# FP4 feed-forward: rounding shared by VectorE and ScalarE, gate and up products in halves around the turning of the tile two behind

## Chip, cores and metric

One core of one Trainium2 chip. The metric is the device time of one execution in microseconds (us); lower is better.

## What is computed

Two transformer layers on 4 x 1024 tokens of width 256, each a residual sum: local attention and a mixture of eight experts, then a delta-rule attention and a feed-forward with weights and activations rounded to FP4. The change touches the last of the four only:

```python
def fp4_quant_dequant(x):                     # blocks of 16 along the last dim
    xb = x.reshape(shape[:-1] + (shape[-1] // 16, 16))
    scale = jnp.maximum(jnp.max(jnp.abs(xb), axis=-1, keepdims=True) / 6.0, 1e-12)
    xn = xb / scale
    idx = jnp.searchsorted(_MID, jnp.abs(xn)) # 0, .5, 1, 1.5, 2, 3, 4, 6
    return (_GRID[idx] * jnp.sign(xn) * scale).reshape(shape)

def fp4_linear(x, w):
    return jnp.einsum('bsk,nk->bsn', fp4_quant_dequant(x), fp4_quant_dequant(w))
...
x = x + _L1_ffn_ref(_layernorm(x, axis=-1), L1_ffn_w_gate, L1_ffn_w_up, L1_ffn_w_down)
# _L1_ffn_ref: fp4_linear(silu(fp4_linear(x, w_gate)) * fp4_linear(x, w_up), w_down); 704 hidden columns
```

## The kernel before

`fp4_feed_forward` first runs the three earlier stages and then its own block, with one instruction list for each engine; semaphores tie the lists together, and each list runs in the order written. The weights have been rounded and packed before. The 4096 tokens are 32 tiles of 128 tokens (`NT`), in 8 trips of 4 (`TRIPS`, `UN`); the tiles of a trip are called tile 0 to 3 here, and n counts tiles through all trips.

Once a trip, for all four tiles together (1024 columns, "wide"): VectorE takes the statistics of the next trip's input (`norm`, L1961, after the hidden product of tile 0), GpSimd the reciprocal root (L1929), VectorE normalises and finds block scales, ratio, exponent and `zmagic` (`round_z`, L1972 to L1988, after tile 1), and GpSimd adds `zmagic`, subtracts it and multiplies by the scale (L1931 to L1935). Adding and subtracting a number of the right size rounds the ratio to FP4's steps. TensorE turns the rounded tiles against the identity (`transpose_z`, L2064, in tile 3) and ScalarE copies them out of PSUM (`copy_zT`).

For each tile n: TensorE makes the gate and up products in two halves of 352 columns (`gate_up`, L2074); ScalarE takes the silu of each half (`silus`); VectorE multiplies silu and up (`hidden`, L1990) and rounds the 704 columns to FP4 (`round_h`, with `fp4`, L1942 to L1959: nine instructions, each waiting for the one ahead). TensorE turns the rounded tile in six pieces (`transpose_h`, L2086), ScalarE copies it out (`copy_hT`), TensorE multiplies by the down weights (`down`, L2095) and VectorE adds the residual into y (`result`, L2002), which the sync queue stores. TensorE's list is: gate and up of n, turning of n - 1, down product of n - 1. VectorE's is: result of n - 2, hidden of n, rounding of n. All is 32-bit float; in the traces each such product stands as two matmul instructions.

Of the kernel before, what the change touches and what calls it, by code (L numbers as in the profile page):

```python
# [14 lines left out]
P = 128  # L15
D = 256
# [1840 lines left out]
def fp4_feed_forward(nc, x_in, consts, w, x_out, T, I):  # L1857
# [21 lines left out]
    with ExitStack() as stack:  # L1879
# [42 lines left out]
        @block.gpsimd  # L1922
        def _(pool):
            pc = Chain(pool, pool_chain)
            blocks = lambda a: a.rearrange("p (b e) -> p b e", e=FP4_BLOCK)
            pool.wait_ge(loaded, 32)
            for t in range(TRIPS):
                pool.wait_ge(var_ready, t + 1)
                nc.gpsimd.tensor_tensor(rstd[:], ve[:], mhalf[:].to_broadcast([P, UN]), ALU.pow).then_inc(rstd_ready, 1)  # L1929
                pool.wait_ge(z_scaled, t + 1)  # L1930
                pc.link(nc.gpsimd.tensor_tensor(zlevel[:], zratio[:], zmagic[:], ALU.add))  # L1931
                pc.link(nc.gpsimd.tensor_tensor(zlevel[:], zlevel[:], zmagic[:], ALU.subtract))
                if t > 0:
                    pool.wait_ge(zT_psum, t * 2)
                nc.gpsimd.tensor_tensor(blocks(qz[:].rearrange("p u d -> p (u d)")), blocks(zlevel[:]),  # L1935
                                        zscl[:].unsqueeze(2).to_broadcast([P, WIDE // FP4_BLOCK, FP4_BLOCK]), ALU.mult).then_inc(qz_ready, 1)

        @block.vector
        def _(dve):
            c = Chain(dve, chain)  # L1940

            def fp4(n, cols, src, out, done, after_read=None):  # L1942

                nb = cols // FP4_BLOCK
                blocks = lambda a: a.rearrange("p (b e) -> p b e", e=FP4_BLOCK)
                per_block = lambda a: a[0:n, 0:nb].unsqueeze(2).to_broadcast([n, nb, FP4_BLOCK])
                r, e, mg, l = ratio[0:n, 0:cols], expo[0:n, 0:cols], magic[0:n, 0:cols], level[0:n, 0:cols]
                c.link(nc.vector.tensor_reduce(amax[0:n, 0:nb], blocks(src), AX, ALU.max, apply_absolute_value=True))  # L1948
                c.link(nc.vector.tensor_scalar(scl[0:n, 0:nb], amax[0:n, 0:nb], 1.0 / FP4_MAX, 1e-12, ALU.mult, ALU.max))
                c.link(nc.vector.reciprocal(inv[0:n, 0:nb], scl[0:n, 0:nb]))  # L1950

                ins = nc.vector.scalar_tensor_tensor(blocks(r), blocks(src), TIES_DOWN, per_block(inv), ALU.mult, ALU.mult)  # L1952
                c.link(ins)
                c.link(nc.vector.tensor_scalar(e.bitcast(U32), r.bitcast(U32), EXPONENT, None, ALU.bitwise_and))  # L1954

                c.link(nc.vector.tensor_scalar(mg, e, 1.0, HALF_STEP, ALU.max, ALU.mult))  # L1956
                c.link(nc.vector.tensor_tensor(l, r, mg, ALU.add))  # L1957
                c.link(nc.vector.tensor_tensor(l, l, mg, ALU.subtract))  # L1958
                nc.vector.tensor_tensor(blocks(out), blocks(l), per_block(scl), ALU.mult).then_inc(done, 1)  # L1959
# [12 lines left out]
            def round_z(t):  # L1972
                dve.wait_ge(rstd_ready, t + 1)
                for u in range(UN):
                    ins = nc.vector.tensor_scalar(z[:, u, :], x[:, t % XB, u, :], mv[:, u, 0:1], rstd[:, u:u + 1], ALU.subtract, ALU.mult)  # L1975
                c.link(ins)
                if t > 0:
                    dve.wait_ge(qz_ready, t)
                nb = WIDE // FP4_BLOCK
                blocks = lambda a: a.rearrange("p (b e) -> p b e", e=FP4_BLOCK)  # L1980
                src = blocks(z[:].rearrange("p u d -> p (u d)"))
# [3 lines left out]
                c.link(nc.vector.scalar_tensor_tensor(blocks(zratio[:]), src, TIES_DOWN, inv[:].unsqueeze(2).to_broadcast([P, nb, FP4_BLOCK]), ALU.mult, ALU.mult))  # L1985
                c.link(nc.vector.tensor_scalar(expo[:].bitcast(U32), zratio[:].bitcast(U32), EXPONENT, None, ALU.bitwise_and))
                nc.vector.tensor_scalar(zmagic[:], expo[:], 1.0, HALF_STEP, ALU.max, ALU.mult).then_inc(z_scaled, 1)
                dve.wait_ge(z_scaled, t + 1)  # L1988

            def hidden(n):  # L1990
                for j in range(2):
                    dve.wait_ge(silu_ready, n * 2 + j + 1)
                    ins = nc.vector.tensor_tensor(h[:, n % 2, j * HI:(j + 1) * HI], silu[:, n % 2, j * HI:(j + 1) * HI], ps_u[j][:, 0:HI], ALU.mult)  # L1993
                    ins.then_inc(h_ready, 1)
                dve.wait_ge(h_ready, n * 2 + 2)

            def round_h(n):
                if n >= 2:
                    dve.wait_ge(hT_psum, n - 1)
                fp4(P, I, h[:, n % 2, :], qh[:, n % 2, :], qh_ready)  # L2000

            def result(n):  # L2002
                t, u = divmod(n, UN)
                dve.wait_ge(y_psum, n + 1)
                if t > 0:
                    dve.wait_ge(stored[u], 16 * t)
                nc.vector.tensor_tensor(y[:, u, :], ps_y[:, 0:D], x[:, t % XB, u, :], ALU.add).then_inc(y_ready, 1)

            norm(0)
            round_z(0)  # L2010
# [10 lines left out]
            result(NT - 2)  # L2021
            result(NT - 1)

        @block.scalar
        def _(act):
# [6 lines left out]
            def silus(n):  # L2032
                if n >= 2:
                    act.wait_ge(h_ready, 2 * n - 2)
                for j in range(2):
                    act.wait_ge(gu_psum, n * 2 + j + 1)
                    nc.scalar.activation(silu[:, n % 2, j * HI:(j + 1) * HI], ps_g[j][:, 0:HI], ACT.Silu).then_inc(silu_ready, 1)
# [9 lines left out]
            for p in range(2):  # L2047
                copy_zT(0, p)
            for n in range(NT):
                t, u = divmod(n, UN)  # L2050
                silus(n)
                if n >= 1:
                    copy_hT(n - 1)
                if u == 3 and t + 1 < TRIPS:
                    for p in range(2):
                        copy_zT(t + 1, p)
            copy_hT(NT - 1)

        @block.tensor
        def _(pe):  # L2060
# [3 lines left out]
            def transpose_z(t):  # L2064
                for p in range(2):
                    pe.wait_ge(qz_ready, t + 1)
                    pe.wait_ge(zT_ready, t * 2 + p)
                    for u in (2 * p, 2 * p + 1):
                        for k in range(KD):
                            col = ((u - 2 * p) * KD + k) * P  # L2070
                            ins = nc.tensor.transpose(ps_z[:, col:col + P], qz[:, u, k * P:(k + 1) * P], ident[:])
                    ins.then_inc(zT_psum, 1)

            def gate_up(n):  # L2074
                t, u = divmod(n, UN)
                pe.wait_ge(zT_ready, t * 2 + u // 2 + 1)
                for j in range(2):
                    if n >= 1:
# [85 lines left out]
```

## Time and profile before

| | us |
|---|---|
| median of 3 runs | 3606.68 (3600.88 to 3606.81) |
| profiled execution | 3596.48 |
| its span, first to last instruction | 3594.6 |
| mean granted clock of TensorE | 0.952 |
| feed-forward stage in the span | 3200 to 3594.6 |

Busy over the whole span: TensorE 3199.4 us (89%), VectorE 2525.7 (70%), ScalarE 1396.1 (39%), GpSimd 945.4 (26%). These shares mix four stages; the feed-forward has to be read by itself. In the rows PE is TensorE, PEld its weight loads, DVE VectorE, ACT ScalarE, POOL GpSimd; L is a line of the kernel. A granted clock of 1.00 is 2.4 GHz for the whole stretch, 0.50 would be 1.2 GHz. Matmuls overlap in the records, so their pace is read from start to start.

### The profile page before, as it was taken

Reading aid. Unit: us, or ns where it says so; the run is one execution under the profiler, and the core shown is the slowest. Engines: PE = TensorE matmul, PEld = TensorE weight load, DVE = VectorE, ACT = ScalarE, POOL = GpSimd, SP = SyncE. Lnnn points to the kernel's source line nnn. Section 1 sums busy time; section 2 is a strip of 40 time slices with the busy share of each in tenths; the row PEclk is TensorE's granted clock in tenths of the full one; section 3 lists DMA queues with packets and bytes.
Section 4 is the critical chain, followed back from the end, with each engine's and each line's share of the span. In section 5 each row is a group of like instructions: output and inputs, shape, how many; then the busy total and the mean of one; then the engine's idle time right before and its main releaser. Section 6 shows DMA issues by size and latency. Waiting matters only on the chain. (4 is left out here: it accounts for less than half of the span.)

```text
span 3594.6 us, 144990 instructions
## 1 busy us (share of the span) xinstructions
PE 3199.4 (89%) x64390; PEld 2378.8 (66%) x64390; DVE 2525.7 (70%) x5676; ACT 1396.1 (39%) x3203; POOL 945.4 (26%) x1051
## 2 busy tenths in 40 slices
PE   6874999998699999999999999999999999758888
PEld 4654999987466666666666666666666666535555
DVE  6774111121688888888888888888888888729887
ACT  2221222221354554545555455455545545321111
POOL 2244122212222232223223323222332322211110
PEclk9886999999899999999999999999999999979999
DMA  2116666665000000000000000000000000010000
GB/s 66 47 61 204 185 184 191 187 207 175 23 9 10 8 11 9 9 10 9 10 8 11 10 8 11 8 10 8 11 10 8 11 8 8 5 48 17 24 24 14
DMA packets 98187, 168.37 MB, mean 47 GB/s; under 512 B 15400, under 2 KB 71976, under 8 KB 97312
## 3 DMA queue, kind: packets, MB, share of 16 engines
q1 hardware_dynamic: 76976, 136.07, 11.5%
q0 software_dynamic: 19440, 21.97, 4.3%
q8 instruction: 513, 8.40, 1.0%
q10 hardware_dynamic: 1152, 1.06, 0.1%
q14 instruction: 106, 0.87, 0.1%
HBM read 118.86 MB, written 38.09 MB: 44 GB/s over the span
## 5 line engine op out<-in xcount | busy, mean ns | idle before, releaser
L1067 POOL TENSOR_TENSOR da_M<-da_M,da_decay 128x512 f32<-128x512 f32 x256 | 261.3, 1046 | 790.4 <-DVE da_TT L1215 438.7
L1379 ACT COPY da_Ub<-da_U 32x256 f32<-32x256 f32 x1024 | 412.2, 403 | 17.2
L1210 DVE TENSOR_TENSOR da_eGn<-da_eGn,da_z 128x30 f32<-128x30 f32 (+14 forms) x960 | 328.2, 342 | 33.0
L1209 DVE TENSOR_TENSOR da_z<-da_eGn 128x30 f32<-128x30 f32 (+14 forms) x960 | 329.2, 343 | 27.6
L1671 PE MATMUL da_C<-da_Ub,da_Km 128*64 128x256 f32 x2048 | 294.6, 406 | 4.9 <-ACT da_Ub L1379 3.4
L1501 PE MATMUL da_unit<-early_buffer,da_xnT 128*128 128x512 f32 x512 | 284.9, 642 | 9.7 <-DVE da_sp L1151 6.4
L840 PEld LDWEIGHTS le_ps_qkv<-le_scr,le_up 128*128 128x128 f32 x2272 | 265.8, 193 | 4.8 <-ACT le_scr L670 1.8
L840 PE MATMUL le_ps_qkv<-le_scr,le_up 128*128 128x128 f32 x2272 | 267.8, 277 | 1.2 <-ACT le_scr L670 1.2
L1372 ACT COPY da_U<-da_A 128x256 f32<-128x256 f32 x256 | 95.4, 373 | 421.3 <-PE da_A L1642 421.2
L1509 PE MATMUL da_unit<-da_xnT,early_buffer 128*128 128x128 f32 x2048 | 242.2, 277 | 9.9 <-ACT da_eGn L1364 9.9
L1642 PEld LDWEIGHTS da_A<-da_W,da_TT 32*32 32x32 f32 x8192 | 127.5, 106 | 183.6 <-DVE da_W L1228 68.5
L1509 PEld LDWEIGHTS da_unit<-da_xnT,early_buffer 128*128 128x128 f32 x2048 | 233.5, 192 | 17.4 <-ACT da_eGn L1364 17.4
L676 ACT ACTIVATE le_scr<-le_ps_qkv 128x512 f32<-128x512 f32 x142 | 84.8, 597 | 363.4 <-PE le_ps_qkv L840 363.4
L1642 PE MATMUL da_A<-da_W,da_TT 32*32 32x64 f32 x8192 | 169.6, 219 | 62.5 <-DVE da_W L1220 46.2
L373 POOL DMA_INDIRECT moe_acc<-le_scr x71 | 110.4, 1555 | 429.5 <-DVE le_scr L571 405.5
L1060 POOL TENSOR_TENSOR da_v<-da_v,da_norm 128x256 f32<-128x256 f32 x128 | 91.6, 732 | 473.4 <-ACT da_v L1351 473.4
L1671 PEld LDWEIGHTS da_C<-da_Ub,da_Km 128*64 128x64 f32 x2048 | 135.1, 140 | 110.7 <-issue 60.8
L1233 DVE TENSOR_TENSOR da_M<-da_C,da_M 128x512 f32<-128x512 f32 x256 | 174.3, 681 | 27.0 <-PE da_C L1671 26.0
L571 DVE TENSOR_SCALAR le_scr<-le_ps_oT,le_scr 128x256 f32<-128x256 f32 x36 | 17.4, 484 | 236.9 <-PE le_ps_oT L850 236.9
L1194 DVE TENSOR_TENSOR da_gm<-da_unit,da_mask 128x640 f32<-128x640 f32 x128 | 105.1, 821 | 110.4 <-PE da_unit L1587 110.3
L1658 PE MATMUL da_B<-da_U,da_gm 32*32 32x64 f32 x8192 | 165.8, 217 | 17.3 <-ACT da_U L1372 15.6
L571 DVE TENSOR_SCALAR le_scr<-le_ps_o,le_scr 128x256 f32<-128x256 f32 x35 | 16.9, 484 | 221.7 <-PE le_ps_o L850 221.7
(299 smaller groups left out, 7014.3 us busy)
## 6 DMA issues: line engine op xcount, KB each, us to landing
le_up<-in_upT SPq DMA_DIRECT2D x71, 1024.0 KB, 5.0
le_scr<-moe_slots SPq DMA_DIRECT2D x71, 129.0 KB, 4.2
le_down<-in_downT SPq DMA_DIRECT2D x8, 1024.0 KB, 12.3
early_buffer<-in_x SPq DMA_DIRECT2D x16, 256.0 KB, 3.8
moe_acc<-le_y SPq DMA_DIRECT2D x32, 128.0 KB, 2.4
da_x<-moe_acc SPq DMA_DIRECT2D x128, 32.0 KB, 1.8
stream<-da_xz SPq DMA_DIRECT2D x128, 32.0 KB, 1.6
stream<-da_y POOLq DMA_DIRECT2D x128, 32.0 KB, 2.8
```

What stands on the lines that cost most here:

```text
L373: nc.gpsimd.indirect_dma_start(acc[:], bass.IndirectOffsetOnAxis(ap=zs[:, n % ZB, D:D + 1].bitcast(U32), axis=0), ye[:, b, :], None, compu ...
L840: ins = nc.tensor.matmul(ps_up[j][:, f * P:(f + 1) * P], up[:, n % UB, k, (j * HB + f) * P:(j * HB + f + 1) * P], zsT[:, n % 2, k, :], sta ...
L1067: ins = nc.gpsimd.tensor_tensor(st_, st_, decay[:, par, rec, 2 * g:2 * g + 2].rearrange("p a b -> p (a b)").unsqueeze(2).to_broadcast([P, ...
L1209: c.link(tt(t, Xm[:, s + 1:C, s:s + 1].to_broadcast([P, below, s]), Xm[:, s:s + 1, 0:s].to_broadcast([P, below, s]), ALU.mult))
L1210: c.link(tt(Xm[:, s + 1:C, 0:s], Xm[:, s + 1:C, 0:s], t, ALU.add))
L1233: tt(st_, Cp[:], st_, ALU.add).then_inc((s_updated, r_updated)[rec], 1)
L1379: ins = nc.scalar.copy(Ub[rows_of(b), :, :, b, :], U[rows_of(b), rec])
L1501: ins = mm(bank, xnT[:, par, kk, :], wx[:, kk, u // 2, cols], start=(kk == 0), stop=(kk == KD - 1))
L1509: ins = mm(bank[:, hp * P:(hp + 1) * P], wx[:, kk, j, col:col + P], xnT[:, par, kk, :], start=(kk == 0), stop=(kk == KD - 1))
L1642: ins = mm(wu[rw, q_, 2 + rec, j], TT[rw, of_solve(g, q_, rec, j), :], W[rw, rec, q_, j], start=True, stop=True)
L1658: ins = mm(po[rw, q_, 1, j], gm[rw, par, g, q_, (first + j) * C:(first + 1 + j) * C], U[rw, rec, q_, j], start=False, stop=(rec == 1), ski ...
L1671: ins = mm(Cp[feat(q_), j * B * DH:(j + 1) * B * DH], Km[:, g, rec, j, DH * q_:DH * (q_ + 1)], Ub[:, q_, j].rearrange("p b e -> p (b e)"), ...
```

## The change

- GpSimd keeps the reciprocal root and two operations on four columns (`nb`, the negative of mean times reciprocal root). Its three wide operations go to VectorE (`z_levels`).
- ScalarE normalises (`normalised`, four operations a trip). It also makes `above` and `zabove` from the exponents: Relu(exponent x HALF_STEP - HALF_STEP), in place of VectorE's `magic` = max(exponent, 1) x HALF_STEP. VectorE then adds in one instruction (above + HALF_STEP) + ratio, and subtracts likewise.
- The residual is added by TensorE: a product of the identity and x starts the accumulation of the down product, and ScalarE copies the sum to y.
- The rounding is cut in two on VectorE: `exponents(n)` after the hidden product, `levels(n - 1)` between the two halves of the hidden product of n. The wide rounding is cut likewise: `z_exponents` after tile 1, `z_levels` after tile 2.
- TensorE's list becomes: first half of gate and up of n, turning of n - 2, second half, down product of n - 2. Turnings of the normalised input stand on both sides of the down product in tile 3.
- `ratio`, `expo`, `above` and the block scales get two buffers.

```diff
@@ block.vector
+            def z_levels(t):
+                dve.wait_ge(zabove_ready, t + 1)
+                c.link(nc.vector.scalar_tensor_tensor(zlevel[:], zabove[:], HALF_STEP, zratio[:], ALU.add, ALU.add))
+                c.link(nc.vector.scalar_tensor_tensor(zlevel[:], zlevel[:], HALF_STEP, zabove[:], ALU.subtract, ALU.subtract))
...
+                nc.vector.tensor_tensor(in_blocks(qz[:].rearrange("p u d -> p (u d)")), in_blocks(zlevel[:]), per_block(zscl[:], NZ), ALU.mult).then_inc(qz_ready, 1)
...
+            def levels(n):
+                k = n % 2
+                dve.wait_ge(above_ready, n + 1)
...
+                c.link(nc.vector.scalar_tensor_tensor(level[:], above[:, k], HALF_STEP, ratio[:, k], ALU.add, ALU.add))
+                c.link(nc.vector.scalar_tensor_tensor(level[:], level[:], HALF_STEP, above[:, k], ALU.subtract, ALU.subtract))
...
             for n in range(NT):
                 t, u = divmod(n, UN)
-                if n >= 2:
-                    result(n - 2)
-                hidden(n)
-                if u == 0 and t + 1 < TRIPS:
-                    norm(t + 1)
-                round_h(n)
-                if u == 1 and t + 1 < TRIPS:
-                    round_z(t + 1)
+                hidden(n, 0)
+                if n >= 1:
+                    levels(n - 1)
+                hidden(n, 1)
+                exponents(n)
+                if t + 1 < TRIPS:
+                    if u == 0:
+                        norm(t + 1)
+                    elif u == 1:
+                        z_exponents(t + 1)
+                    elif u == 2:
+                        z_levels(t + 1)
@@ block.scalar
+            def steps_above(n):
+                act.wait_ge(expo_ready, n + 1)
+                if n >= 2:
+                    act.wait_ge(qh_ready, n - 1)
+                nc.scalar.activation(above[:, n % 2], expo[:, n % 2], ACT.Relu, bias=below[:], scale=HALF_STEP).then_inc(above_ready, 1)
...
-                silus(n)
-                if n >= 1:
-                    copy_hT(n - 1)
-                if u == 3 and t + 1 < TRIPS:
-                    for p in range(2):
-                        copy_zT(t + 1, p)
+                silus(n, 0)
+                if n >= 2:
+                    copy_hT(n - 2)
+                if u == 2 and more:
+                    z_above(t + 1)
+                silus(n, 1)
+                if u == 1 and more:
+                    normalised(t + 1)
+                if u == 3 and more:
+                    copy_zT(t + 1, 0)
+                if n >= 2:
+                    result(n - 2)
+                if u == 3 and more:
+                    copy_zT(t + 1, 1)
+                steps_above(n)
@@ block.tensor
+                nc.tensor.matmul(ps_y[:, 0:D], ident[:], x[:, (n // UN) % XB, n % UN, :], start=True, stop=False)
                 for k in range(IC):
...
+                turn = u == 3 and t + 1 < TRIPS
+                gate_up(n, 0)
+                if n >= 2:
+                    transpose_h(n - 2)
+                gate_up(n, 1)
+                if turn:
+                    transpose_z(t + 1, 0)
+                if n >= 2:
+                    down(n - 2)
+                if turn:
+                    transpose_z(t + 1, 1)
```

TensorE, one plain tile of the steady trips before: the two halves of gate (ff_ps_g) and up (ff_ps_u), the turning (ff_ps_h) and the down product (ff_ps_y).

```order
L2082 MATMUL ff_ps_g<-ff_packed,ff_zqT 128x352 x2
L2082 MATMUL ff_ps_u<-ff_packed,ff_zqT 128x352 x2
L2082 MATMUL ff_ps_g<-ff_packed,ff_zqT 128x352 x2
L2082 MATMUL ff_ps_u<-ff_packed,ff_zqT 128x352 x2
L2092 MATMUL ff_ps_h<-ff_ident,ff_qh 128x128 x5
L2092 MATMUL ff_ps_h<-ff_ident,ff_qh 64x128
L2101 MATMUL ff_ps_y<-ff_packed,ff_hqT 128x256 x6
```

The same tile with the change:

```order
L2121 MATMUL ff_ps_g<-ff_packed,ff_zqT 128x352 x2
L2121 MATMUL ff_ps_u<-ff_packed,ff_zqT 128x352 x2
L2131 MATMUL ff_ps_h<-ff_ident,ff_qh 128x128 x5
L2131 MATMUL ff_ps_h<-ff_ident,ff_qh 64x128
L2121 MATMUL ff_ps_g<-ff_packed,ff_zqT 128x352 x2
L2121 MATMUL ff_ps_u<-ff_packed,ff_zqT 128x352 x2
L2138 MATMUL ff_ps_y<-ff_x,ff_ident 128x256
L2141 MATMUL ff_ps_y<-ff_packed,ff_hqT 128x256 x6
```

The second half stands between turning and down product, and the product with the identity opens the down product.

VectorE, a tile without wide work, with the change: the halves of the hidden product (ff_h), the levels of the tile ahead between them, then the exponents.

```order
L1978 TENSOR_TENSOR ff_h<-ff_silu,ff_ps_u 128x352
L2000 SCALAR_TENSOR_TENSOR ff_level<-ff_above,ff_ratio 128x704
L2001 SCALAR_TENSOR_TENSOR ff_level<-ff_level,ff_above 128x704
L2004 TENSOR_TENSOR ff_qh<-ff_level,ff_hscl 128x704
L1978 TENSOR_TENSOR ff_h<-ff_silu,ff_ps_u 128x352
L1987 TENSOR_REDUCE ff_amax<-ff_h 128x44
L1988 TENSOR_SCALAR ff_hscl<-ff_amax 128x44
L1989 RECIPROCAL ff_inv<-ff_hscl 128x44
L1990 SCALAR_TENSOR_TENSOR ff_ratio<-ff_h,ff_inv 128x704
L1993 TENSOR_SCALAR ff_expo<-ff_ratio 128x704
```

Ten instructions stand where twelve stood: ff_magic and the residual add are gone.

ScalarE, the same kind of tile, with the change:

```order
L2037 ACTIVATE ff_silu<-ff_ps_g 128x352
L2043 COPY ff_hqT<-ff_ps_h 128x512
L2044 COPY ff_hqT<-ff_ps_h 128x128
L2045 COPY ff_hqT<-ff_ps_h 64x128
L2037 ACTIVATE ff_silu<-ff_ps_g 128x352
L2071 COPY ff_y<-ff_ps_y 128x256
L2058 ACTIVATE ff_above<-ff_expo,ff_below 128x704
```

Before, the two silus stood together ahead of the three copies; now the result's copy and ff_above stand ahead of the next tile's first silu.

## Rows read from the trace of the kernel before

**Rows 1.** Busy time by stretches: start:end, us, PE, PEld, DVE, ACT, POOL, PEclk, DMA.

```profile
3200.00:3229.40 29.40, 9.84 (x29) 6.52 (x30) 8.98 (x22) 3.38 (x5) 7.64 (x4) 0.57 0.36 130
3274.10:3319.30 45.20, 37.28 (x144) 24.91 (x144) 40.73 (x68) 8.44 (x23) 8.18 (x4) 0.96 0.08 24
3229.40:3550.80 321.40, 264.02 (x994) 175.91 (x992) 285.44 (x469) 58.76 (x154) 57.23 (x28) 0.93 0.06 20
3340.00:3352.00 12.00, 10.02 (x20) 6.38 (x21) 11.62 (x14) 0.00 (x0) 7.15 (x3) 0.57 0.03 11
3550.00:3580.00 30.00, 26.24 (x104) 17.57 (x105) 23.56 (x38) 6.22 (x18) 0.00 (x0) 1.00 0.04 14
```

**Rows 2.** Timeline, VectorE: start us, us, engine, line, operation, shapes, count.

```profile
3411.41 1.41 DVE L1965 BATCH_NORM_STATS2 ff_st<-ff_x 128x6 f32<-128x256 f32 x4
...
3413.34 0.88 DVE L1948 TENSOR_REDUCE ff_amax<-ff_h 128x44 f32<-128x704 f32 x1
...
3419.65 0.42 DVE L2007 TENSOR_TENSOR ff_y<-ff_ps_y,ff_x 128x256 f32<-128x256 f32 x1
3419.98 1.02 DVE L1993 TENSOR_TENSOR ff_h<-ff_silu,ff_ps_u 128x352 f32<-128x352 f32 x2
...
3422.64 0.89 DVE L1952 SCALAR_TENSOR_TENSOR ff_ratio<-ff_h,ff_inv 128x704 f32<-128x704 f32 x1
...
3424.12 0.53 DVE L1956 TENSOR_SCALAR ff_magic<-ff_expo 128x704 f32<-128x704 f32 x1
3424.69 0.89 DVE L1957 TENSOR_TENSOR ff_level<-ff_ratio,ff_magic 128x704 f32<-128x704 f32 x1
...
3427.34 1.38 DVE L1975 TENSOR_SCALAR ff_z<-ff_x,ff_mv,ff_rstd 128x256 f32<-128x256 f32 x4
...
3430.83 1.22 DVE L1985 SCALAR_TENSOR_TENSOR ff_zratio<-ff_z,ff_inv 128x1024 f32<-128x1024 f32 x1
...
3432.81 0.69 DVE L1987 TENSOR_SCALAR ff_zmagic<-ff_expo 128x1024 f32<-128x1024 f32 x1
3433.54 0.42 DVE L2007 TENSOR_TENSOR ff_y<-ff_ps_y,ff_x 128x256 f32<-128x256 f32 x1
```

**Rows 3.** Timeline, GpSimd's wide operations and VectorE beside them, same trip.

```profile
3433.59 2.36 POOL L1931 TENSOR_TENSOR ff_zlevel<-ff_zratio,ff_zmagic 128x1024 f32<-128x1024 f32 x1 [19.06 <-DVE ff_zmagic L1987]
...
3438.44 2.46 POOL L1935 TENSOR_TENSOR ff_qz<-ff_zlevel,ff_zscl 128x1024 f32<-128x1024 f32 x1
...
3436.48 2.62 DVE L1952 SCALAR_TENSOR_TENSOR ff_ratio<-ff_h,ff_inv 128x704 f32<-128x704 f32 x1
3439.14 2.14 DVE L1954 TENSOR_SCALAR ff_expo<-ff_ratio 128x704 uint32<-128x704 uint32 x1
```

**Rows 4.** Timeline, TensorE: a plain tile, then the wide turnings; idle before in brackets.

```profile
3414.95 1.45 PE L2082 MATMUL ff_ps_g<-ff_packed,ff_zqT 128*128 128x352 f32 x4
...
3419.78 0.88 PE L2092 MATMUL ff_ps_h<-ff_ident,ff_qh 128*128 128x128 f32 x6
3421.65 3.05 PE L2101 MATMUL ff_ps_y<-ff_packed,ff_hqT 128*128 128x256 f32 x12 [0.99 <-ACT ff_hqT L2045]
3424.64 1.45 PE L2082 MATMUL ff_ps_g<-ff_packed,ff_zqT 128*128 128x352 f32 x4
...
3445.39 0.60 PE L2071 MATMUL ff_ps_z<-ff_ident,ff_qz 128*128 128x128 f32 x4
3447.12 1.07 PE L2071 MATMUL ff_ps_z<-ff_ident,ff_qz 128*128 128x128 f32 x4 [1.13 <-ACT ff_zqT L2030]
```

**Rows 5.** Timeline, TensorE: a down product that waited.

```profile
3341.98 5.76 PE L2101 MATMUL ff_ps_y<-ff_packed,ff_hqT 128*128 128x256 f32 x12 [3.83 <-DVE ff_y L2007]
```

**Rows 6.** Groups of instructions, ScalarE: busy us, mean ns of one, idle before.

```profile
L1335 ACT ACTIVATE da_sp<-da_sp 128x1024 f32<-128x1024 f32 x64 | 67.5, 1056 | 1.7
...
L636 ACT ACTIVATE early_buffer<-le_y,le_nb,le_rstd 128x256 f32<-128x256 f32 x64 | 33.2, 592 | 39.2 <-POOL le_nb L345 39.2
L2037 ACT ACTIVATE ff_silu<-ff_ps_g 128x352 f32<-128x352 f32 x64 | 29.7, 464 | 264.4 <-PE ff_ps_u L2082 264.4
```

More of the change, by code:

```diff
@@ L1924, in _ @@
             pc = Chain(pool, pool_chain)
-            blocks = lambda a: a.rearrange("p (b e) -> p b e", e=FP4_BLOCK)
+            nc.gpsimd.memset(below[:], -HALF_STEP).then_inc(made, 1)
+            pc.link(nc.gpsimd.memset(neg[:], -1.0))
             pool.wait_ge(loaded, 32)
@@ L1940, in _ @@
             c = Chain(dve, chain)
[L1942 to L1959, printed above, removed]
             def norm(t):
@@ L1990, in hidden @@
[L1990 to L1997, printed above, removed]
+                c.link(nc.vector.scalar_tensor_tensor(in_blocks(zratio[:]), src, TIES_DOWN, per_block(inv[:], NZ), ALU.mult, ALU.mult))
@@ L2002, in result @@
[L2002 to L2007, printed above, removed]
+                nc.vector.tensor_tensor(in_blocks(qh[:, k, :]), in_blocks(level[:]), per_block(hscl[:, k], NB), ALU.mult).then_inc(qh_ready, 1)
             norm(0)
-            round_z(0)
+            z_exponents(0)
@@ L2024, in _ @@
+            levels(NT - 1)
         @block.scalar
@@ L2030, in copy_zT, with silus @@
                 nc.scalar.copy(zqT[:, t % 2, 2 * p:2 * p + 2].rearrange("p u k t -> p (u k t)"), ps_z[:]).then_inc(zT_ready, 1)
-            def silus(n):
+            def silus(n, j):
                 if n >= 2:
[L2034 to L2037, printed above, removed]
+                    act.wait_ge(h_ready, 2 * n - 3 + j)
+                act.wait_ge(gu_psum, n * 2 + j + 1)
+                nc.scalar.activation(silu[:, n % 2, j * HI:(j + 1) * HI], ps_g[j][:, 0:HI], ACT.Silu).then_inc(silu_ready, 1)
             def copy_hT(n):
@@ L2045, in copy_hT, with normalised @@
                 nc.scalar.copy(hqT[0:I - 5 * P, n % 2, 5, :], ps_h[1][0:I - 5 * P, P:2 * P]).then_inc(hT_ready, 1)
-            for p in range(2):
-                copy_zT(0, p)
+            def normalised(t):
+                act.wait_ge(nb_ready, t + 1)
+                if t > 0:
+                    act.wait_ge(zexpo_ready, t)
+                for u in range(UN):
+                    nc.scalar.activation(z[:, u, :], x[:, t % XB, u, :], ACT.Identity, bias=nb[:, u:u + 1], scale=rstd[:, u:u + 1]).then_inc(z_ready, 1)
@@ L2049, in _, with result @@
+            def result(n):
+                t, u = divmod(n, UN)
+                act.wait_ge(y_psum, n + 1)
+                if t > 0:
+                    act.wait_ge(stored[u], 16 * t)
+                nc.scalar.copy(y[:, u, :], ps_y[:, 0:D]).then_inc(y_ready, 1)
+            act.wait_ge(made, 1)
+            normalised(0)
+            z_above(0)
+            copy_zT(0, 0)
+            copy_zT(0, 1)
             for n in range(NT):
                 t, u = divmod(n, UN)
-                silus(n)
@@ L2052, in _ @@
-                if n >= 1:
-                    copy_hT(n - 1)
-                if u == 3 and t + 1 < TRIPS:
-                    for p in range(2):
-                        copy_zT(t + 1, p)
-            copy_hT(NT - 1)
+                more = t + 1 < TRIPS
+                silus(n, 0)
[6 more added lines that the diff above has]
+                    normalised(t + 1)
@@ L2059, in _ @@
+                if u == 3 and more:
[5 more added lines that the diff above has]
+                steps_above(n)
+            for n in (NT - 2, NT - 1):
+                copy_hT(n)
+                result(n)
         @block.tensor
```

128 lines of the change are left out of this document (69 added, 59 removed).

## Prediction

> **What bounds the kernel now.** I read the busy table by stretches first, to find how much of the time the diff can touch. The feed-forward is the last stage: it begins at 3200 us of a span of 3594.6, so about 395 us are in play and 3200 are not. Of these, 29.4 us are start-up, and seven like trips of four tiles fill 321.4 us, 45.9 a trip [rows 1]. In a trip of 45.2 us VectorE is busy 40.7, TensorE 37.3, ScalarE 8.4 and GpSimd 8.2 [rows 1]: VectorE is the fullest engine, TensorE close behind, and neither is full, so each waits for the other somewhere.
>
> Next the timeline of VectorE. A plain tile, from its residual add to the start of what follows it, takes 3419.65 to 3427.34, 7.69 us without a wait [rows 2]. The rounding of the normalised input, once a trip, takes 3427.34 to 3433.54, 6.20 us, and the statistics 3411.41 to 3413.34, 1.93 us [rows 2]. Beside GpSimd's three wide operations two VectorE instructions grow: ff_ratio takes 2.62 us where it takes 0.89 elsewhere [rows 2, 3], and ff_expo 2.14 [rows 3], where an operation of the same kind and width, ff_magic, takes 0.53 [rows 2]. That is 1.73 + 1.61 = 3.3 us a trip that belongs to the neighbour. So VectorE's trip is 4 x 7.69 + 6.20 + 1.93 + 3.3 = 42.2 us, and the missing 3.7 us up to 45.9 are waits.
>
> Then TensorE. A plain tile repeats after 3424.64 - 3414.95 = 9.69 us, of which 0.99 is a wait for ScalarE's copy of the turned tile, which stands directly between turning and down product [rows 4]. Once a trip TensorE is held 3.83 us at the down product by VectorE's late residual add; there the same twelve matmuls took 5.76 us [rows 5] where they take 2.99 (3421.65 to 3424.64, [rows 4]), and the granted clock of that stretch was 0.57, its lower level of 1.2 GHz for most of it, against 1.00 where TensorE had only the short waits [rows 1]. So about 2 to 3 us of some trips are a consequence of VectorE's delay.
>
> **The change, part by part.**
>
> *VectorE's tile.* ff_magic goes to ScalarE (0.57 from its start to the next start) and the residual add goes to TensorE (3419.65 to 3419.98, 0.33) [rows 2]: 7.69 - 0.57 - 0.33 = 6.79 us. The two additions become three-operand instructions. The nearest row is ff_ratio, the same kind at the same width, 0.89, and plain additions take 0.89 too [rows 2], so I cost the new form at nothing. The bounds: nothing below, and above, doubled, 0.9 us an instruction; that end is a rival below.
>
> *VectorE's wide rounding.* The normalising (1.38 + 0.03) and ff_zmagic (0.69 + 0.04) leave; three operations come from GpSimd, each like ff_zratio, 1.22 + 0.04 [rows 2]: 6.20 - 1.41 - 0.73 + 3.8 = 7.9 us. GpSimd's wide work is gone, and with it the 3.3 us of growth.
>
> *Sum for VectorE:* 4 x 6.79 + 7.9 + 1.93 = 37.0 us a trip, 5.2 less than before.
>
> *A new wait.* VectorE's exponents of tile n go to ScalarE, which computes ff_above and only then reaches the first silu of tile n + 1; VectorE's next instruction waits for that silu. silu is 0.46 for 352 columns and a 1024-wide operation 1.06 [rows 6], which puts the 704-wide step at about 0.8 by a straight line between them (an estimate); the relay is then 0.8 + 0.46 and little else, 1.3 us. After tile 0 it is covered by the statistics, after tile 1 and 2 by the halves of the wide rounding (4.1 and 3.8 us). After tile 3 nothing covers it. VectorE: 37.0 + 1.3 = 38.3. Bounds: 0, if VectorE is ahead and waits for TensorE anyway, and 4 x 1.3, if no cover holds.
>
> *TensorE.* Between the turning of tile n - 2 and its down product now lie the second half of gate and up, 2.4 us, half of 3414.95 to 3419.78 [rows 4], so ScalarE's copy no longer holds the engine: 9.69 - 0.99 = 8.70. The residual comes in as one more matmul of 256 columns through the identity. Twelve instructions for six such products take 2.99 us [rows 4], so it costs 0.50: 9.20 a tile. The eight turnings of the normalised input cost 2 x 0.60 at the full clock, and the 1.13 us between their halves [rows 4] now lie under the down product. TensorE: 4 x 9.20 + 1.2 = 38.0 us a trip. The long hold by the residual add goes too: the bank of the result is freed by ScalarE, one tile earlier in the pipeline, so I expect the clock to stay at its full level.
>
> *ScalarE.* It takes on the four normalisings (0.59 each [rows 6]), the steps (4 x 0.8), one 1024-wide step (1.06) and four result copies, about 8 us on top of 8.4. At some 17 of 38 us it isn't full; what counts is its order. The result copy of tile n - 2 stands ahead of ff_above of tile n and waits for the down product. That product ends about 3.5 us (2.99 + 0.50) behind the second half of gate and up; VectorE's exponents, which ff_above needs anyway, end some 0.5 + 0.5 + 3.1 = 4.1 us behind the same point (silu, half product, and 3421.0 to 3424.12 for the exponents [rows 2, 6]). The product is just in time, so this costs nothing; if it were late, VectorE would wait.
>
> *GpSimd and the queues.* Two tiny operations on four columns per trip, far from any bound: they have from tile 0 to tile 1. Every store on the sync queue waits for a result one tile later than before; the load of x behind it is wanted three tiles later. Nothing.
>
> *Start and end.* At the start the first wide rounding lies bare: GpSimd's 2.36, some 2.4 (what lies between the two rows) and 2.46 [rows 3] and ff_zmagic 0.7 leave, and three VectorE operations (3.8), ScalarE's step (1.1), 0.7 more for normalising there and two small GpSimd operations (about 0.4, an estimate) come: -1.9. At the end two tiles instead of one remain to be turned and multiplied: about +1.
>
> A rule against the change, which the sum does without: the Trainium skill, page "ScalarE: Activation LUTs", section "Rules for kernel authors", says to put relu, add and multiply on VectorE and not on ScalarE. Taken for one instruction the rows agree: 0.53 on VectorE, about 0.8 on ScalarE. By the rule the step would stay, and VectorE's trip would be 37.0 + 4 x 0.57 + 0.73 = 40.0 with no relay, 1.7 us above the 38.3 of my sum; the rule counts an instruction, and here the engine is what is short.
>
> **The sum.** VectorE 38.3, TensorE 38.0; I take 38.3 a trip. 7 x (45.9 - 38.3) = 53.2, and 1.9 - 1 at the ends: 54 us less. The profiled execution took 3596.48 us (span 3594.6), so it would become 3542. The median of the runs is 3606.68, 10 us higher; the same gain from it gives 3553. I forecast between, 3548 us.
>
> **The rivals.**
>
> 1. *Neither engine gets through unheld* (chance 0.16). Two engines at 38 us a trip each, coupled by three waits a tile, seldom both run full; if the relay is bare after every tile, VectorE's trip is 37.0 + 4 x 1.3 = 42.2, and the gain 7 x 3.7 + 1 = 27 us: about 3575. For it: before, the engines lost 3.7 us a trip to each other. Against: the two-tile distance leaves TensorE over 5 us of slack before it needs a hidden half.
>
> 2. *Slower: the three-operand addition with two full-width tensors* (0.04). ff_ratio's second operand is a broadcast of 44 numbers; no row shows this kind with two full streams. If each took double, a trip would gain 8 x 0.89 + 2 x 1.22 = 9.6 us: 38.3 + 9.6 = 47.9, 14 us more in seven trips, about 3615. It decides from 45.9: some 1.6 us for 704 columns. Against: plain additions with two full streams take 0.89 as well [rows 2].
>
> 3. *The change takes work off, but the time stays* (0.03): a trip is held by a chain through all three engines that the busy table doesn't show; then within 0.2% of 3600. Against: plain stretches at 9.69 a tile, in which only ScalarE's copy held TensorE [rows 4].
>
> 4. *TensorE alone sets the pace and the identity product hides* (0.07): 37.3 a trip, 61 us less, about 3541; it lies in the forecast's own range.
>
> **How the numbers follow.** The forecast with rival 4 has 0.77, 3532 to 3566; rival 1 reaches to 3576. The range that leaves out 2 in 10 is 3534 to 3574. A measurement of this kernel tells apart about 0.2%, 7 us. Faster: 0.77 + 0.16, with a little off for mishaps not listed, 0.92; same 0.03; slower 0.05.
>
> **What would show it.** Right: trips of 37.5 to 39 us in the feed-forward; ff_ratio at 0.89 everywhere; no wait of the down product for ScalarE's copies; a granted clock near 1.00 from the second trip; VectorE's only regular wait, of about 1.3 us, for the silu after tile 3; the three-operand additions at 0.9 and 1.2. Wrong: those additions above 1.5 us (rival 2); a wait for silu after every tile (rival 1); a lower clock in steady trips; ScalarE's result copy ending later than VectorE's exponents.

## The result and the profile after

The changed kernel took 3543.98 us (median of 4 runs, 3542.56 to 3548.32); the kernel before, 3606.74 (3600.88 to 3612.45). The ratio is 0.9828 with a 95% interval of 0.9811 to 0.9845: 63 us faster. The forecast was 3548.

The profiled execution took 3542.56 us (span 3540.8), where the sum gave 3542. That is partly luck, as the spans show. The feed-forward began, by its first statistics, at 3202.2 us of the profiled execution before and at 3208.8 of the one after: the three untouched stages took 6.6 us longer. In the profiles of the experiments below, all with the same earlier stages, the point lies anywhere from 3203.8 to 3218.9. So I judge by the stage's own length, from its first statistics to the end of the span: 392.4 us before, 332.0 after, 60.4 less.

The busy table by stretches after the change (start:end, us, PE, PEld, DVE, ACT, POOL, PEclk, DMA): the start, a steady trip, three steady trips, the whole stage.

```profile
3208.80:3237.00 28.20, 11.97 (x35) 7.83 (x36) 12.25 (x23) 6.60 (x10) 1.44 (x3) 0.60 0.30 109
...
3356.90:3394.40 37.50, 36.32 (x154) 25.31 (x153) 34.93 (x59) 16.09 (x37) 1.97 (x3) 1.00 0.10 29
3314.47:3426.81 112.34, 108.81 (x458) 75.79 (x457) 104.62 (x173) 48.12 (x105) 5.91 (x9) 1.00 0.09 29
3208.80:3540.80 332.00, 297.56 (x1216) 205.97 (x1216) 279.71 (x456) 129.91 (x281) 15.49 (x24) 0.96 0.09 31
```

Against the trips of [rows 1]: 37.45 us in place of 45.9 (112.34 / 3), TensorE busy 36.3 of it instead of 37.3 of 45.2, GpSimd 2.0 instead of 8.2, and the granted clock 1.00, its upper level of 2.4 GHz, throughout.

VectorE's timeline of a steady trip, from the first half of the wide rounding (after tile 1) to the next trip's statistics, to be held beside [rows 2]:

```profile
3360.44 1.21 DVE L1961 TENSOR_REDUCE ff_amax<-ff_z 128x64 f32<-128x1024 f32 x1
...
3364.37 0.51 DVE L1978 TENSOR_TENSOR ff_h<-ff_silu,ff_ps_u 128x352 f32<-128x352 f32 x1
3364.80 0.88 DVE L2000 SCALAR_TENSOR_TENSOR ff_level<-ff_above,ff_ratio 128x704 f32<-128x704 f32 x1
3365.72 0.89 DVE L2001 SCALAR_TENSOR_TENSOR ff_level<-ff_level,ff_above 128x704 f32<-128x704 f32 x1
...
3370.53 0.53 DVE L1993 TENSOR_SCALAR ff_expo<-ff_ratio 128x704 uint32<-128x704 uint32 x1
3370.98 1.22 DVE L1969 SCALAR_TENSOR_TENSOR ff_zlevel<-ff_zabove,ff_zratio 128x1024 f32<-128x1024 f32 x1
...
3374.75 0.52 DVE L1978 TENSOR_TENSOR ff_h<-ff_silu,ff_ps_u 128x352 f32<-128x352 f32 x1
...
3380.92 0.53 DVE L1993 TENSOR_SCALAR ff_expo<-ff_ratio 128x704 uint32<-128x704 uint32 x1
3382.75 0.52 DVE L1978 TENSOR_TENSOR ff_h<-ff_silu,ff_ps_u 128x352 f32<-128x352 f32 x1 [1.30 <-ACT ff_silu L2037]
...
3389.36 1.40 DVE L1947 BATCH_NORM_STATS2 ff_st<-ff_x 128x6 f32<-128x256 f32 x4
...
3391.29 0.51 DVE L1978 TENSOR_TENSOR ff_h<-ff_silu,ff_ps_u 128x352 f32<-128x352 f32 x1
```

It is one dense line with a single gap: 1.30 us, after tile 3, for the silu. ScalarE's timeline shows what it waited for: ff_above first, and the silu behind it. The first row is a silu after tile 1, where ScalarE was free and only TensorE's product was waited for.

```profile
3361.86 0.46 ACT L2037 ACTIVATE ff_silu<-ff_ps_g 128x352 f32<-128x352 f32 x1 [0.42 <-PE ff_ps_u L2121]
...
3381.48 0.89 ACT L2058 ACTIVATE ff_above<-ff_expo,ff_below 128x704 f32<-128x704 f32 x1 [1.62 <-DVE ff_expo L1993]
3382.28 0.44 ACT L2037 ACTIVATE ff_silu<-ff_ps_g 128x352 f32<-128x352 f32 x1
```

TensorE in the same trip, to be held beside [rows 4]: a tile's first half, the turning, the second half, the identity product (L2138), the down product, the next tile, the wait ahead of the wide turning, and the up product of the next trip's first half.

```profile
3359.13 1.45 PE L2121 MATMUL ff_ps_g<-ff_packed,ff_zqT 128*128 128x352 f32 x4
3360.42 1.35 PE L2121 MATMUL ff_ps_u<-ff_packed,ff_zqT 128*128 128x352 f32 x4
3361.60 0.82 PE L2131 MATMUL ff_ps_h<-ff_ident,ff_qh 128*128 128x128 f32 x6
3362.26 1.35 PE L2121 MATMUL ff_ps_g<-ff_packed,ff_zqT 128*128 128x352 f32 x4
...
3364.63 0.59 PE L2138 MATMUL ff_ps_y<-ff_x,ff_ident 128*128 128x256 f32 x2
3365.06 2.95 PE L2141 MATMUL ff_ps_y<-ff_packed,ff_hqT 128*128 128x256 f32 x12
3367.94 1.45 PE L2121 MATMUL ff_ps_g<-ff_packed,ff_zqT 128*128 128x352 f32 x4
...
3374.77 0.66 PE L2111 MATMUL ff_ps_z<-ff_ident,ff_qz 128*128 128x128 f32 x4 [1.18 <-DVE ff_qz L1973]
...
3380.26 1.35 PE L2121 MATMUL ff_ps_u<-ff_packed,ff_zqT 128*128 128x352 f32 x4
```

The down product no longer waits for ScalarE's copy; the 1.18 us for VectorE's wide rounding is TensorE's only wait in the trip. Where only the up product is waited for, the silu starts 1.44 us behind that product's start (3360.42 to 3361.86). By this the silu after tile 3 could have started at about 3381.7 (an estimate); it started at 3382.28, behind ff_above. So TensorE's chain to that silu ends about 0.6 us ahead of ScalarE's step.

### The profile page after: what moved, and what is told of

It is laid out like the page before. It is cut to its first block and busy times, and to the rows that moved or that the text cites. A ratio compares the mean times of both kernels' runs of the same rounds, so it can differ in the third digit from the quotient of the medians.

```text
span 3540.8 us, 145315 instructions
## 1 busy us (share of the span) xinstructions
PE 3201.8 (90%) x64454; PEld 2387.4 (67%) x64454; DVE 2482.4 (70%) x5596; ACT 1457.2 (41%) x3307; POOL 895.8 (25%) x1045
```

## The experiments

The table has, for each kernel, the stage and a steady trip; both are read from the starts of the statistics, which come once a trip.

| kernel | stage, us | steady trip, us |
|---|---|---|
| before | 392.4 | 45.2 and 46.9 |
| changed | 332.0 (333.0 in a second profile) | 37.45 |
| e4, changed without the residual product | 333.6 | 37.4 to 38.0 |
| e2, changed, residual add on VectorE | 338.9 | 38.44 |
| e1, changed, step on VectorE | 354.5 | 40.99 |
| e3, changed, wide rounding on GpSimd | 363.5 | 41.5 to 42.0 |
| e8, before with the new order alone | 384.6 | 43.8 to 44.1 |
| e9, changed with old order, rounding in one piece | 381.9 | 44.1 |
| e5, changed with TensorE's old order | 432.4 | 49.1 to 52.5 |
| e6 and r2, changed, wide work spread | 322.9 (both) | 36.25 |

**Which engine sets the pace: the residual left out, or given back.** The first edit takes four products a trip from TensorE and touches VectorE not at all.

```diff
-                nc.tensor.matmul(ps_y[:, 0:D], ident[:], x[:, (n // UN) % XB, n % UN, :], start=True, stop=False)
...
-                    ins = nc.tensor.matmul(ps_y[:, 0:D], hqT[0:width, n % 2, k, :], downT[0:width, k, :], start=False, stop=(k == IC - 1))
+                    ins = nc.tensor.matmul(ps_y[:, 0:D], hqT[0:width, n % 2, k, :], downT[0:width, k, :], start=(k == 0), stop=(k == IC - 1))
```

> The changed kernel without the product of the identity and x; the output lacks the last residual. Measured by the steady trip of the feed-forward, 37.45 us in the changed kernel. Theory A, VectorE sets the pace (36.15 us of work and one bare wait of 1.30 a trip): the trip stays at 37.4 to 37.5. Theory B, TensorE sets it: 4 x 0.43 us leave the engine and the trip falls to about 35.7, the stage by 12 us.

Measured: 37.43 in every second trip, 37.8 and 38.0 in those between; the stage 333.6, 1.6 longer. TensorE has 1.7 us a trip less to do, and no trip gets shorter. Its wait ahead of the wide turning grew from 1.18, to 1.92 in the short trips and 2.89 in the long ones:

```profile
3371.03 0.66 PE L2111 MATMUL ff_ps_z<-ff_ident,ff_qz 128*128 128x128 f32 x4 [1.92 <-DVE ff_qz L1973]
...
3333.02 1.11 PE L2111 MATMUL ff_ps_z<-ff_ident,ff_qz 128*128 128x128 f32 x4 [2.89 <-DVE ff_qz L1973]
...
3341.57 0.52 DVE L1978 TENSOR_TENSOR ff_h<-ff_silu,ff_ps_u 128x352 f32<-128x352 f32 x1 [1.88 <-ACT ff_silu L2037]
```

The long trips are the clock's: behind the wait of 2.89 us the granted clock was 0.68 (3333.00 to 3338.00), the wide turning took 1.11 for 0.66, and VectorE's wait after tile 3 became 1.88 for 1.30. Behind the wait of 1.92 it stayed at 1.00 (3371.00 to 3376.00). Theory A holds: VectorE, with its one wait, sets the pace. In the second edit the same add goes to VectorE instead (`result`, written as in the kernel before).

```diff
...
             for n in range(NT):
                 t, u = divmod(n, UN)
+                if n >= 3:
+                    result(n - 3)
                 hidden(n, 0)
...
```

> The changed kernel with the residual add back on VectorE, at the head of each tile for the tile three behind; TensorE without the identity product, ScalarE without the result's copy. Theory A, VectorE sets the pace: 4 x 0.33 more, a trip of 38.8 us, the stage 9 us longer. Theory B, TensorE sets it: 4 x 0.43 less, 35.7 us.

Measured: 38.44 a trip and a stage of 338.9, 7 longer. The sign and size are A's; 38.8 was 0.4 high because the wait after tile 3 shrank, to 0.96 or 1.18 us:

```profile
3390.67 0.52 DVE L1978 TENSOR_TENSOR ff_h<-ff_silu,ff_ps_u 128x352 f32<-128x352 f32 x1 [0.96 <-ACT ff_silu L2049]
```

**The step back on VectorE, no longer on ScalarE.**

```diff
...
-                nc.vector.tensor_scalar(expo[:, k].bitcast(U32), ratio[:, k].bitcast(U32), EXPONENT, None, ALU.bitwise_and).then_inc(expo_ready, 1)
+                c.link(nc.vector.tensor_scalar(expo[:, k].bitcast(U32), ratio[:, k].bitcast(U32), EXPONENT, None, ALU.bitwise_and))
+                nc.vector.tensor_scalar(above[:, k], expo[:, k], 1.0, HALF_STEP, ALU.max, ALU.mult).then_inc(above_ready, 1)
...
-                steps_above(n)
...
```

> The changed kernel with the step (max of exponent and 1, times a constant) back on VectorE, for the tiles and for the wide rounding, nothing else moved. Theory A: 4 x 0.57 + 0.73 more work, and the bare wait of 1.30 for ScalarE goes: 36.15 + 3.0 = 39.2 us a trip, the stage 12 to 14 us longer. Rival, the rule that such operations belong on VectorE and the round trip to ScalarE costs more than it saves: 37.4 or less.

Measured: 40.99, 1.8 above theory A's 39.2. VectorE's work is 39.1, theory A's, but a wait after tile 3 of 1.87 us is there although ScalarE has no step left:

```profile
3390.15 0.52 DVE L1980 TENSOR_TENSOR ff_h<-ff_silu,ff_ps_u 128x352 f32<-128x352 f32 x1 [1.87 <-ACT ff_silu L2038]
```

TensorE's timeline in this kernel shows another chain to the same silu: the wide turning waits for VectorE's ff_qz of tile 2, and down product, second wide turning and the first half follow it in the list. The last row is the busy table of that stretch.

```profile
3381.04 0.66 PE L2108 MATMUL ff_ps_z<-ff_ident,ff_qz 128*128 128x128 f32 x4 [3.04 <-DVE ff_qz L1975]
3381.53 0.90 PE L2135 MATMUL ff_ps_y<-ff_x,ff_ident 128*128 128x256 f32 x2
3382.23 4.38 PE L2138 MATMUL ff_ps_y<-ff_packed,ff_hqT 128*128 128x256 f32 x12
3386.53 0.65 PE L2108 MATMUL ff_ps_z<-ff_ident,ff_qz 128*128 128x128 f32 x4
...
3381.00:3386.60 5.60, 5.56 (x19) 4.09 (x20) 5.37 (x9) 0.59 (x1) 0.00 (x0) 0.70 0.00 0
```

Behind that wait of 3.04 us the granted clock was 0.70. From identity product to second wide turning it took 5.00 us (3381.53 to 3386.53), where the changed kernel, at 1.00, takes 3.31 (3375.27 to 3378.58). Those 1.69 us are nearly the whole wait of 1.87: at the upper level about 0.2 of it would be left and the trip would be about 39.3 (an estimate), theory A's. So the bare wait of the changed kernel has two causes, ScalarE's step and, 0.6 us ahead of it, TensorE's chain, and my forecast knew the first.

The Trainium skill, page "ScalarE: Activation LUTs", section "Rules for kernel authors", says to put relu, add and multiply on VectorE. For one instruction the rows agree: 0.53 us there, 0.88 on ScalarE. Here, where VectorE is the engine that is short, moving the step there made the trip 3.5 us longer: about 1.8 by VectorE's longer list less the wait, and 1.7 by the lower clock that followed.

**The wide rounding back on GpSimd, no longer on VectorE.**

```diff
...
+                pool.wait_ge(zabove_ready, t + 1)
+                pc.link(nc.gpsimd.tensor_tensor(zlevel[:], zratio[:], zabove[:], ALU.add))
+                pc.link(nc.gpsimd.tensor_tensor(zlevel[:], zlevel[:], zabove[:], ALU.subtract))
...
-                    elif u == 2:
-                        z_levels(t + 1)
...
```

> The changed kernel with the wide rounding's three operations back on GpSimd (and the wide step on VectorE, 0.73). VectorE: 36.15 - 3.8 + 0.73 = 33.1, and two bare waits of 1.3 (after tile 2 and 3). Theory A, VectorE is slowed beside GpSimd by 3.3 us a trip as before: 33.1 + 2.6 + 3.3 = 39.0 us a trip; ff_ratio or the additions in that stretch at 2 us and more. Rival, the growth belonged to the order of before and not to GpSimd: 35.7, held up by TensorE at about 36.3.

Measured: 41.5 to 42.0, longer than either theory gave. The timelines of GpSimd and VectorE in one trip:

```profile
3417.04 2.36 POOL L1938 TENSOR_TENSOR ff_zlevel<-ff_zratio,ff_zabove 128x1024 f32<-128x1024 f32 x1 [9.13 <-DVE ff_zabove L1977]
3419.48 2.88 POOL L1939 TENSOR_TENSOR ff_zlevel<-ff_zlevel,ff_zabove 128x1024 f32<-128x1024 f32 x1
3422.43 2.46 POOL L1942 TENSOR_TENSOR ff_qz<-ff_zlevel,ff_zscl 128x1024 f32<-128x1024 f32 x1
...
3417.00 0.52 DVE L1991 TENSOR_TENSOR ff_h<-ff_silu,ff_ps_u 128x352 f32<-128x352 f32 x1
3417.43 2.71 DVE L2013 SCALAR_TENSOR_TENSOR ff_level<-ff_above,ff_ratio 128x704 f32<-128x704 f32 x1
3420.18 2.92 DVE L2014 SCALAR_TENSOR_TENSOR ff_level<-ff_level,ff_above 128x704 f32<-128x704 f32 x1
3423.14 2.50 DVE L2017 TENSOR_TENSOR ff_qh<-ff_level,ff_hscl 128x704 f32<-128x704 f32 x1
```

Three VectorE instructions grow by 5.5 us, against the 3.3 that two grew by before. With it 33.1 + 2.6 + 5.5 = 41.2 is the trip of 41.5 but for 0.3; in the trip of 42.0 the second bare wait is 1.81. The growth is not a fixed factor: by the profile's spans for GpSimd, each grown instruction ends 0.74 or 0.75 us behind the end of the GpSimd operation beside it (3420.14 behind 3419.40, 3423.10 behind 3422.36, 3425.64 behind 3424.89), so it takes what is left of that operation and most of its own 0.89. Before, the first of GpSimd's operations (3433.59 to 3435.95, [rows 3]) lay beside instructions that did not grow: the two halves of ff_h, with an operand in PSUM, and ff_amax, with one operand (1.02 and 0.88 in [rows 2]):

```profile
3433.88 0.94 DVE L1993 TENSOR_TENSOR ff_h<-ff_silu,ff_ps_u 128x352 f32<-128x352 f32 x2
3434.86 0.89 DVE L1948 TENSOR_REDUCE ff_amax<-ff_h 128x44 f32<-128x704 f32 x1
```

The Trainium skill, page "GPSIMD Engine Reference", section "Key points", says that GpSimd shares its SBUF interfaces with VectorE and contends with instructions of two SBUF inputs and those in a two-port mode. The trace agrees for the three that grow, which have two SBUF inputs each, and for the two kinds that don't; which mode an instruction runs in no run here shows.

**Order and load, each alone.** Three kernels take the change apart. The first is the kernel before with the new lists for TensorE and for ScalarE's silus and copies; VectorE's residual add moves one tile later with them.

```diff
...
-                gate_up(n)
-                if n >= 1:
-                    transpose_h(n - 1)
+                gate_up(n, 0)
+                if n >= 2:
+                    transpose_h(n - 2)
+                gate_up(n, 1)
...
```

> The kernel before with TensorE's new order alone: first half of gate and up of n, turning of n - 2, second half, down product of n - 2; the residual add on VectorE for the tile three behind; VectorE, GpSimd and the rounding as before. Theory A, VectorE's work of 42.2 us a trip (with 3.3 of growth beside GpSimd) is then the pace: 42 to 43 us, the stage 22 to 27 us shorter than before, without the slow clock in steady trips. Rival, the order is the gain by itself: 37 to 39 us a trip.

Measured: 43.8 to 44.1. Theory A's pace, a little above; the gain of the stage, 7.8 us, is far below the 22 I gave, because the first trip behind the start took 48.1 us and the five behind it save 2.0 each (43.9 on average for 45.9). VectorE sets the pace here: a trip of 43.78 less the one wait for a silu in it, 1.64, is 42.1, the sum's 42.2. TensorE now waits for VectorE's residual add seven times in three trips, 20.6 us in all, and the clock of steady trips stayed at 0.94: my "without the slow clock" was wrong. The wait of VectorE, the waits of three trips (us in total, times, longest) and their busy table:

```profile
3417.76 0.52 DVE L1993 TENSOR_TENSOR ff_h<-ff_silu,ff_ps_u 128x352 f32<-128x352 f32 x1 [1.64 <-ACT ff_silu L2038]
...
PE ff_ps_y L2104 <- DVE ff_y L2007: 20.6, 7, 5.2
...
3330.78:3462.20 131.42, 110.79 (x434) 75.05 (x433) 121.74 (x202) 25.22 (x66) 24.52 (x12) 0.94 0.08 25
```

The second has VectorE's light work of the changed kernel, still split, with TensorE's old list.

```diff
...
-                gate_up(n, 0)
-                if n >= 2:
-                    transpose_h(n - 2)
-                gate_up(n, 1)
+                gate_up(n, 0)
+                gate_up(n, 1)
+                if n >= 1:
+                    transpose_h(n - 1)
...
```

> The changed kernel with TensorE's old order: both halves of gate and up of tile n, then turning and down product of tile n - 1 (ScalarE's copies in the same order, its step ahead of the result's copy). VectorE's work is that of the changed kernel. Theory A: TensorE again waits 0.99 us for ScalarE's copy and about 1.5 us for VectorE's levels, which start only after the first half's silu: 4.84 + 1.5 + 0.66 + 0.99 + 3.31 = 11.3 us a tile, 45 to 46 a trip, nearly all of the gain lost. Rival, the lighter VectorE is the gain by itself: 37.5 to 39.5 us a trip.

Measured: 49.1 to 52.5, slower than before the change. TensorE's timeline in this kernel has both waits in every tile:

```profile
3384.50 0.87 PE L2131 MATMUL ff_ps_h<-ff_ident,ff_qh 128*128 128x128 f32 x6 [1.46 <-DVE ff_qh L2004]
3386.37 0.70 PE L2138 MATMUL ff_ps_y<-ff_x,ff_ident 128*128 128x256 f32 x2 [0.99 <-ACT ff_hqT L2045]
...
3396.24 0.87 PE L2131 MATMUL ff_ps_h<-ff_ident,ff_qh 128*128 128x128 f32 x6 [1.46 <-DVE ff_qh L2004]
```

A tile takes 11.74 us here (11.3 expected) at the full clock (1.00 in 3384.50 to 3396.24). The granted clock over three trips was 0.92, and VectorE waited 43.4 us in them for silus. Four such tiles are 47 us; the rest up to 49.1 to 52.5 is the wide turnings and stretches at the lower clock. The split rounding hands its levels over half a product late; in the changed kernel, with the distance of two tiles, no steady trip has a wait for them.

The third rounds a tile in one piece again: exponents, a wait for ScalarE's step, levels.

```diff
...
                 hidden(n, 0)
-                if n >= 1:
-                    levels(n - 1)
                 hidden(n, 1)
...
                 exponents(n)
+                levels(n)
...
```

> The changed kernel's lighter VectorE in the old order altogether: TensorE with both halves, then turning and down product of n - 1, and VectorE's rounding of a tile in one piece again (exponents, a wait for ScalarE's step, levels). Theory A: the light rounding without the new order is held by TensorE's 8.81 + 0.99 us a tile and by VectorE's waits for the step: 41 to 43.5 us a trip, the stage 15 to 30 us shorter than before (392.4). Rival, the split rounding is what made the one-behind order bad and the load is the whole gain: 37.5 to 39.5. A second rival, the load is worth nothing without the order: 45 to 47.

Measured: 44.1 in most trips, 0.6 above the range; the stage 381.9, 10.5 shorter than before, below my 15 to 30. The down product waits 0.99 us for ScalarE's copy and the wide turning 2.4 us for VectorE. VectorE in turn waits 0.95 us in every tile for ScalarE's step, which the kernel before has on VectorE. The waits of three trips (us in total, times, longest):

```profile
DVE ff_level L2000 <- ACT ff_above L2056: 11.4, 12, 0.9
...
PE ff_ps_y L2136 <- ACT ff_hqT L2043: 8.9, 9, 1.0
...
PE ff_ps_z L2109 <- DVE ff_qz L1973: 7.1, 3, 2.4
```

The order alone is worth 7.8 us, the load with the old order and an unsplit rounding 10.5, the whole change 60.4. Each part alone runs into waits for another engine. The 10.5 belong to this load, with its step on ScalarE: a lighter list without that wait was not run. Nor was the new order with the new load and an unsplit rounding, so what the split is worth by itself stays open; with the old order it cost 50.5 us (e5 against e9).

**A better version: the wide work spread over four tiles.**

```diff
...
+                if u == 3 and t + 2 < TRIPS:
+                    norm(t + 2)
                 if t + 1 < TRIPS:
                     if u == 0:
-                        norm(t + 1)
+                        z_exponents(t + 1)
                     elif u == 1:
-                        z_exponents(t + 1)
+                        z_rounded(t + 1)
                     elif u == 2:
-                        z_levels(t + 1)
+                        z_scaled(t + 1)
...
```

`z_rounded` holds the two additions of `z_levels` and `z_scaled` its product with the scales; ScalarE's `normalised` and `z_above` move up one tile with them.

> The changed kernel with VectorE's wide work spread over all four tiles: the statistics two trips ahead after tile 3, the exponents after tile 0, the two additions after tile 1, the scaling after tile 2, so that each wait for ScalarE's step has work in front of it. Theory A: the bare wait of 1.30 us goes; VectorE 36.15, TensorE 4 x 8.81 + 1.0 = 36.24: 36.2 to 36.5 us a trip, the stage 6 to 8 us shorter than that of the changed kernel (332.0). Rival, the wait is of TensorE's making and comes back elsewhere: 37.4, nothing gained.

Measured: steady trips of 36.25 to 36.27 and a stage of 322.9, 9.1 shorter than the changed kernel's (6 to 8 expected); 3537.65 us (3530.98 to 3543.55), ratio to before 0.9803 (0.9780 to 0.9826), which overlaps the changed kernel's 0.9828. The stage began at 3218.9 in this profile, so both kernels went to one chip together:

> The changed kernel as it is, for comparison on one chip with the next run: steady trips of 37.45 us and a stage of 332 us whatever the earlier stages take.

> The kernel with VectorE's wide work spread over all four tiles once more, beside the changed kernel on the same chip: steady trips of 36.26 us, a stage 8 to 10 us shorter than the changed kernel's. A rival, that what is gained in the stage is lost ahead of it (its stage began 10 us later than the changed kernel's in the profiles): the stage begins as late again and the whole is no faster.

Measured: the changed kernel 3545.88 us (3541.34 to 3549.90), ratio 0.9829 (0.9815 to 0.9842), stage 333.0, begun at 3211.1; the spread version 3530.94 (3526.84 to 3539.13), ratio 0.9787 (0.9773 to 0.9801), stage 322.9, begun at 3214.4. It is 15 us faster, of which 10 stand in the stage; the other 5 are not shown to be the change's, since each stage was profiled in one run, for the spread version in its slowest. The intervals of the two ratios don't meet, and the late start of its profiles did not cost it the gain. Three steady trips of the second, same columns as above:

```profile
3306.93:3415.69 108.76, 108.76 (x458) 75.78 (x457) 104.34 (x173) 47.85 (x105) 5.91 (x9) 1.00 0.09 30
```

TensorE is busy 108.76 of 108.76 us. VectorE, with 0.23 us of waiting a trip in the first profile of this version, is as good as full too. What remains is work to be taken off both.

## Why the prediction was right

- **VectorE sets the pace, at 38.3 a trip.** Right; 37.45. Its terms, measured: the plain tile 6.61 (3364.37 to 3370.98) for 6.79, the wide halves 3.93 (3360.44 to 3364.37) and 3.77 (3370.98 to 3374.75) for 7.9 together, the statistics 1.93 for 1.93, the bare wait 1.30 for 1.3. The tile was over-sized by 0.18, four times a trip.
- **The three-operand additions cost nothing.** Right: 0.88 and 0.89 at 704 columns, 1.22 at 1024; rival 2 falls.
- **A bare wait after tile 3 only.** Right in place and size, through a longer step than I took: ff_above is 0.88 us, not 0.8. My straight line ran through rows without a column of biases. The Trainium skill, page "ScalarE: Activation LUTs", section "What ACT_TABLE_LOAD costs", gives 280 + 0.833 N ns with such a column, by estimate 0.87 us for 704. The trace agrees. It didn't matter, since the silu starts 0.80 behind the step's start. That a chain through TensorE ends only 0.6 us ahead of it I had not seen, nor that behind a longer wait of TensorE ahead of the wide turning the clock is lower and that chain the later one (e1, e4).
- **TensorE, 38.0 a trip.** Over-sized by 1.7: a tile takes 8.81 (3359.13 to 3367.94) for 9.20. The identity product is 0.43 for 0.50. The larger part: taking the wait for the copy away freed 1.3 us and not the 0.99 of [rows 4], for from turning to next product it was 1.87 (3419.78 to 3421.65) and is 0.66 now, and the down product itself went from 2.99 to 2.88. VectorE being the bound, this error cost the forecast nothing.
- **ScalarE's result copy ahead of ff_above.** Right that it costs nothing, and with more room than the 0.6 us of the sum: in the steady trip ff_above waited for VectorE's exponents after every tile, 0.95 to 2.68 us, the copy done.
- **The clock.** Right for the steady trips, 1.00, against 0.93 over the trips before [rows 1]. It came later than "from the second trip": between the second and third statistics (3238.17 to 3276.75) it was 0.91, with a wait of 3.07 us ahead of the first wide turning in it.
- **GpSimd's neighbourhood, 3.3 us.** Right for the kernel before, whose trip with the new order is 42.1 and one wait (e8); with other instructions beside GpSimd it is 5.5 (e3).
- **The ends.** From the first statistics to the first product, 18.2 us for 19.4: -1.2, forecast -1.9. The tail was 1 us longer by forecast and came out 1 us shorter: from the first product of the last trip to the end it was 49.4 for 50.4 before. The sign was wrong.
- **The sum.** Seven trips gave 58 us, not 53: 8.3 each. The stage became 60 shorter, not 54, and the median run 63. The profiled execution showed the 54 of the sum only because the earlier stages took 6.6 us more in it. That the median lies 4 us from the forecast is in part luck too: the forecast lies between two bases, 3542 and 3553, and the sum under it was 6 us short. The direction of the error was one: both engines' tiles were priced too long.
- **Rival 1** (waits between the engines eat the gain) fell at this distance and this order; e8, e9 and e5 show it where one half of the change is missing. Rival 3 fell with the stage's 60 us. Rival 4's trip of 37.3 is nearer to the measured 37.45 than the sum's 38.3, but by chance: it equals TensorE's busy time of before [rows 1], where the sum's terms without the identity product give 4 x 8.70 + 1.2 = 36.0. TensorE has its floor at 36.25 (r2), and it was not the one that set the pace (e4).

## What to carry to other kernels

Where two engines are both nearly full and wait for each other, lighten the one and lengthen the distance between them in the same change, and price the pair: here two partial changes gave 8 and 10 us and the whole 60. Price an operation by the engine that is short, not by the engine that does it fastest. When one gap a trip is left, look for small work that can be spread in front of it, and check what second chain ends close to it.

## What the runs showed that I had not expected

A short wait of TensorE can cost more than its idle time: 0.99 us idle by the profile, where the ends of matmuls are modelled, and 1.3 us gained when it went. A longer one can cost more still: behind waits of 2.89 (e4) and 3.04 us (e1) the granted clock was 0.68 and 0.70 over the next 5 to 6 us, and what followed took 1.7 us longer in e1, so that taking work off TensorE (e4) made some trips longer. Beside GpSimd's wide float operations a VectorE instruction with two SBUF tensors ends only about 0.74 us behind GpSimd's operation (2.71, 2.92 and 2.50 us for 0.89), GpSimd's own take up to 2.88 for 2.34, and a product with one operand in PSUM is left alone. And the untouched stages ahead end anywhere in 3202 to 3219 us, which is as much as the last improvement is worth: a stage has to be compared with the stage.
